# A two-layer gated cross-attention block on one core: the order of transposing turns in one DMA queue

## The reference

```python
x = x + tanh(g_xattn[0]) * L0_xattn(layernorm(x), ctx)      # stage 1: single-head cross-attention
x = x + tanh(g_ffn[0])   * L0_ffn(layernorm(x))             # stage 2: ternary feed-forward
x = x + tanh(g_xattn[1]) * L1_xattn(layernorm(x), ctx, ..)  # stage 3: 16-head cross-attention
x = x + tanh(g_ffn[1])   * L1_ffn(layernorm(x))             # stage 4: FP4 (nvfp4) feed-forward
# L0_ffn: h = gelu(rmsnorm(x) @ ternary(w_up).T); rmsnorm(h) @ ternary(w_down).T     (512 -> 2048 -> 512)
# L1_ffn: h = silu(q(x) @ q(gate).T) * (q(x) @ q(up).T); q(h) @ q(down).T, q = FP4 codes with a scale per 16
```

## Time and profile before

| | |
|---|---|
| median of 3 runs | 1825.38 us (1817.82 to 1830.28) |
| the profiled execution's own time | 1823.66 us |
| its span in the trace | 1821.9 us |
| PE busy | 1371.2 us (75% of the span) |
| DVE busy | 1421.6 us (78%) |
| ACT busy | 692.5 us (38%) |
| POOL busy | 243.9 us (13%) |
| mean granted TensorE clock | 0.892 of full speed |
| busy share of the 16 DMA engines in q1, which holds all of the kernel's transfers | 26.5% |

### The profile page before, as it was taken

One profiled execution on the slowest core, in us unless ns is written; L12 is line 12 of the kernel. 1 busy time (PEld: TensorE's weight loads), 2 busy tenths in 40 slices (PEclk: granted clock), 3 DMA queues, 4 the chain that ended last, 5 costly groups with the idle time before them and its releaser, 6 DMA issues.

```text
span 1821.9 us, 24307 instructions
## 1 busy us (share of the span) xinstructions
PE 1371.2 (75%) x8120; PEld 705.4 (39%) x8120; DVE 1421.6 (78%) x2437; ACT 692.5 (38%) x2105; POOL 243.9 (13%) x197
## 2 busy tenths in 40 slices
PE   5044737799787978698778978797869886988663
PEld 4021315344453436344543345343634453434321
DVE  6988896878787687787787878768777778786695
ACT  2112206451455227441644146422734164425310
POOL 1102200131003200230013100320013001310000
PEclk9556868899889989999999989998999999999888
DMA  9175761042101420233004210142023300420012
GB/s 348 68 243 146 188 143 36 6 88 64 42 1 35 93 59 14 35 62 77 25 7 87 58 48 1 35 93 59 14 35 65 75 24 6 87 58 24 7 24 51
DMA packets 267433, 120.08 MB, mean 66 GB/s; under 512 B 244090, under 2 KB 244602, under 8 KB 265750
## 3 DMA queue, kind: packets, MB, share of 16 engines
q1 hardware_dynamic: 267286, 118.27, 26.5%
HBM read 49.04 MB, written 8.39 MB: 32 GB/s over the span
## 4 chain that ended last, share of the span: by engine, by line
issue 43%; DVE 26%; PE 18%; DMA 4%; SPq 4%; ACT 3%; POOL 2%; POOLq 0%; DVEq 0%; ACTq 0%
PE bank L1075 13%; PE bank L1164 5%; DVE amax L826 2%; DVE pair L835 2%; DVE hid L831 2%; SPq L314 2%; DVE th L868 2%; SPq L303 1%; DVE pair L850 1%; DMA region<-region 1%; ACT region L535 1%; DVE pair L843 1%; DMA hqt<-pair 1%; DVE sc L797 1%; DVE stats L686 1%
## 5 line engine op out<-in xcount | busy, mean ns | idle before, releaser
L1164 PE MATMUL bank<-w_dn,region 128*128 128x512 fp8e4 x1024 | 243.7, 386 | 40.0 <-DMA region<-region 40.0
L1075 PE MATMUL bank<-w_up,xt 128*128 128x512 fp8e4 x1024 | 248.6, 391 | 32.7 <-ACT region L499 17.4
L1075 PE MATMUL bank<-w_gate,xqt 128*128 128x512 bf16 x512 | 147.9, 416 | 122.2 <-DVE th L868 78.4
L508 ACT ACTIVATE th<-bank,half_cg 128x512 f32<-128x512 f32 x128 | 88.0, 687 | 350.2 <-PE bank L1075 350.2
L426 POOL TENSOR_TENSOR region<-g,region 128x512 f16<-128x512 f32 x128 | 178.9, 1402 | 300.9 <-ACT region L499 292.9
L868 DVE SCALAR_TENSOR_TENSOR th<-th,bank 128x512 f32<-128x512 f32 x128 | 87.6, 684 | 138.4 <-ACT th L508 138.3
L535 ACT ACTIVATE region<-bank,nm 128x77 f32<-128x77 f32 x512 | 160.0, 345 | 68.2 <-DVE nm L914 68.2
L1075 PE MATMUL bank<-w_down,hqt 128*128 128x512 bf16 x512 | 134.3, 422 | 56.9 <-DMA hqt<-pair 56.9
L496 ACT ACTIVATE g<-bank 128x512 f32<-128x512 f32 x128 | 76.4, 597 | 247.2 <-PE bank L1075 188.2
L1164 PEld LDWEIGHTS bank<-w_dn,region 128*128 128x128 f16 x1024 | 101.0, 99 | 167.4 <-issue 52.0
L1075 PEld LDWEIGHTS bank<-w_up,xt 128*128 128x128 f16 x1024 | 102.0, 101 | 163.5 <-issue 55.4
(11 more groups left out here) (206 smaller groups left out, 2473.6 us busy)
## 6 DMA issues: line engine op xcount, KB each, us to landing
xin<-in_x SPq DMA_DIRECT2D x16, 512.0 KB, 4.1
out_x<-x SPq DMA_DIRECT2D x16, 512.0 KB, 3.0
region<-in_w_up_t SPq DMA_DIRECT2D x1, 4096.0 KB, 12.9
hid<-in_gate_w SPq DMA_DIRECT2D x4, 1024.0 KB, 5.2
x<-in_gate_w SPq DMA_DIRECT2D x4, 1024.0 KB, 6.1
hid<-in_up_w SPq DMA_DIRECT2D x4, 1024.0 KB, 5.2
x<-in_up_w SPq DMA_DIRECT2D x4, 1024.0 KB, 5.8
hid<-in_down_w SPq DMA_DIRECT2D x4, 1024.0 KB, 4.9
```

Of the source, the lines that this page charges most:

```text
L508: eng.activation(th[:, u % 2, :], bank[4][:, :], ACT.Tanh, scale=half_cg[:, :]).then_inc(sg["th"], 1)
L1075: last = mm(out, lhs, rhs, start=(n == 0), stop=(n == len(pairs) - 1))
L1164: last = mm(bank[2 + t % 2][:, :], ht[i][:, t % 2, f, :], w_dn[:, f, :], start=(f == 0 and i == 0), stop=(f == KF - 1 and i == 1))
```

## The change

In `turns`, which writes the order of SP's queue for a pass, the turn of the first feed-forward's tile 1 is moved ahead of the first code turn `turn_h(g, 0)`, and that of tile 3 ahead of the second one, `turn_h(g, 1)`. Tiles 0 and 2 keep their places. Nothing is added or removed, and no other engine's list changes.

```diff
                 if g1 is not None:
                     turn_ht(g1, 0)
+                    turn_ht(g1, 1)
                 turn_h(g, 0)
                 if g1 is not None:
-                    turn_ht(g1, 1)
                     turn_ht(g1, 2)
+                    turn_ht(g1, 3)
                 turn_h(g, 1)
-                if g1 is not None:
-                    turn_ht(g1, 3)
                 store(g, 0)
```

## The result

| | before | after |
|---|---|---|
| median of 16 runs each | 1821.7 us (1815.69 to 1834.56) | 1810.06 us (1806.84 to 1815.98) |
| the profiled execution's span | 1821.9 us | 1807.6 us |
| mean granted TensorE clock | 0.892 | 0.905 |
| PE busy | 1371.2 us | 1353.0 us |
| DVE busy | 1421.6 us | 1422.8 us |

The ratio is 0.9933 with a 95% interval of 0.9915 to 0.9952. Forecast were 1821 us with a range of 1813 to 1830, a gain of 4.2 us, and 0.95 for staying within 1%. The gain was 11.6 us: still within 1%, but the time lies outside the range, and the gain is nearly three times the 4.2 us of the forecast.

What follows compares the result with a forecast made beforehand. It took a chain going to and fro between PE and DVE to bound the kernel; removing six slot 12 waits gave 1825.4 - 4.2 = 1821 us against the median, with 1813 to 1830 us 8 times in 10.

Steps and rivals of the forecast that it cites:

- the place and the number of the waits: PE's slot 12, first quarter of tile 1's down: six waits of 0.35 to 0.67 us, one per pass except pass 7.
- the second move costs and brings nothing that shows: SP's queue: code turn 1 behind tile 3's turn still lands 5.8 us before PE's slot 20 needs it; cost nothing.
- The size of the term: Slot 12: six waits adding to 3.27 us, plus 6 x 0.15 us for modelled matmul ends, 4.2 us in all.
- Does the end see it? ... I take the whole 4.2 us: Behind slot 12: PE runs in order and DVE, ACT and POOL follow it, so the end gains the full 4.2 us.
- the bounds of 0 and 4.2 us: Gain from slot 12: between 0, if swallowed at some later wait, and the whole 4.2 us.
- The term that the sum had at nothing: PE's clock behind slot 12: by the rows, short waits cost no clock, so filling them gives nothing more.
- The rule weighed: Matmuls back to back keep PE's clock up: filling slot 12 would give at most 2.3 us a pass, 14 us; rows say nothing.
- A late code turn 1: SP's queue behind tile 3's turn, PE's slot 20: 2 us late in each of seven passes, 1835 us; chance 0.04.
- Rival 3: Single instructions last 0.7 us longer or shorter; over seven passes 5 us, 1816 or 1826 us; chance of exceeding the gain 0.12.
- Rival 4: Slot 12: the filled gap also gives back clock, 14 us, 1807 us; chance 0.01.
- The longest such issue was used as a bound: SP's transposes of tile 1: with the longest issue, 3.7 us, and landing, 5.8 us, ready at 391.3, 10 us spare.

Runs made afterwards that it cites:

- before_fill3: Kernel before the change, with 3 matmuls into an unread bank on PE in slot 12 ahead of down, where it waited; 1824.24 us, 0.9999 of before.
- after_five: Changed kernel plus unread matmuls: 12 before gate product fourteen, 16 before tile 3's down4, 8 in attention step 2, 3+3 in steps 18/19, 6 before first up; 1793.61 us.
- after_busy3: Changed kernel with 3 matmuls into an unread bank on PE in slot 12, where it no longer waits; 1827.85 us, 1.0021 of before.
- before_shift: Kernel before the change, with 40 short matmuls (80 instructions) on PE ahead of stage 4's first gate product; 1838.84 us, 1.0077 of before.

## Why the prediction was wrong

**Right**: the place and the number of the waits, that only the six in slot 12 count, that the first move removes them and nothing else waits instead (36.8 us in 3 pieces; I had written about 36.7). Right too that the second move costs and brings nothing that shows: code turn 1 was issued 3.4 us behind its codes instead of 0.1 and was in time. The size of the term holds roughly in the stretches B, 3.1 us in six of them for the pair of traces, against 4.2.

**The step that failed** is "Does the end see it? ... I take the whole 4.2 us", with the bounds of 0 and 4.2 us. It treats what stands behind slot 12 as rigid: shifted, but as long as before. The trace that I had shows that it isn't, beyond the few rows that I had read. In the kernel before the stretches between the same two events last 96 to 103 us, and the runs spread over 12.5 us; I put this spread down to measurement. Much of it goes with the clock, as the executions above show, and the clock hangs on timing: a pass shorter by 0.6 us brought stretches A of 98 and 100 us in place of 98 to 103. That is where some 7 of the 12 us are, and the upper bound of the sum was no bound. The term that the sum had at nothing, the clock behind slot 12, measured 7.6 us in the pair of traces.

**The rule weighed** was asked the wrong question. I looked whether the clock falls in slot 12; it doesn't, and before_fill3 shows that filling that gap gives nothing (1824.2 us). The clock falls in other waits, which the change never touches but moves, and how long it stays down differs from pass to pass. After the same wait of 4.86 us for tile 3's code turn, PE's 16 matmuls in the changed kernel take 6.58 us in one pass and 4.98 us in another (the latter's wait 4.85 us), and behind the 1.40 us that after_five leaves of it 3.63 us:

```profile
866.60 6.58 PE L1074 MATMUL bank<-w_down,hqt 128*128 128x512 bf16 x16 [4.86 <-DMA hqt<-pair]
```

```profile
1064.40 4.98 PE L1074 MATMUL bank<-w_down,hqt 128*128 128x512 bf16 x16 [4.85 <-DMA hqt<-pair]
```

```profile
674.80 3.63 PE L1074 MATMUL bank<-w_down,hqt 128*128 128x512 bf16 x16 [1.40 <-DMA hqt<-pair]
```

The Trainium skill (Perfetto Trace Analysis, Matmul Optimizations) asks for matmuls back to back because the engine scales its power with its use. after_five agrees for the waits of A: with work in them the granted clock is 1.00 there, and the time was 18 us less.

**The rivals.** A late code turn 1 didn't happen. Rival 3, small shifts of either sign, came nearest in form, but I had priced it at 5 us, and for meetings of DVE and POOL; the shifts were larger and the clock's. Rival 4, the clock, had a chance of 0.01 and came nearest in number, with 1807 us. That is in part luck: its mechanism, the filled gap of slot 12, is the one that before_fill3 refutes, and its 14 us came from another wait. But it named the right cost, and the rows against it spoke only of slot 12.

**A cause that was only half named.** The prediction laid the wait to the queue's order, with the 3.49 us of the first issue in the very chain that it quoted. The longest such issue was used as a bound, and why it was that long was not asked. In these traces the wait needs both: the old order and an instruction fetch in that issue. Where either was missing, slot 12 didn't wait.

**Open.** Whose fetch it is was not tested by itself, but the traces speak for PE: q8 has 10 packets in each of the first five passes of the kernel before and of every kernel with at most 12 instructions more on PE, and 11 in all those with 80 or more, and only PE's list was changed between them. By what exactly the timing decides how long the clock stays down was not measured, and so which change of a pass's length helps can't be forecast from these runs. That the change of length acts through the clock is shown by where the time lies and by the two kernels with added matmuls in slot 12; it isn't shown by a pair that differs in the wait alone while the clock is held, since each of the three kernels of the old order with work in the waits lost its wait in the loop as well. So the bare wait's price at an even clock is known only roughly, from the stretches B.

## What to carry to other kernels

Where a loop repeats and PE waits some microseconds in each pass, cut the trace at one event per pass and compare the lengths and granted clocks of the same stretch before summing anything: if they differ, a small edit elsewhere can be worth several times its own size, with either sign, and the range has to hold that. Such a kernel can gain more from work placed in PE's long waits (18 us here, in the third version tried) than from a wait of half a microsecond removed. Test a suspected wait by putting its time back as work. And when a control is meant to hold one thing and leave another, look in its trace whether it did: with work in the waits the two orders, 11 us apart before, were 0 to 3.5 us apart, but the old one had lost its wait too.

## What the runs showed of the hardware

- The length of the same stretch of program went with the granted clock: 98 us at 0.95 to 0.96, 100 at 0.93, 103 to 104 at 0.88 to 0.90, and 95.6 at 1.00 with 14 matmuls more in PE's waits there (after_five). Adding 0.65 us of work a pass moved a kernel from the mixture of 98 and 100 to one with 100 and 104 (after_busy3, 1827.85 us).
- A packet of the instruction queue q8 that falls into the issue of a transposing DMA of 128x2048 went with an issue of 3.0 to 3.7 us, where the others took at most 2.5 us (kernel before, 8 and 56 issues). Pass after pass it met the same issue; 80 instructions added on PE moved it away, 8 did not. A packet that only touched the beginning or the end of an issue left it short (1.6 us in the changed kernel).
- The order of PE's and SP's lists is thus not all that sets their timing: adding instructions to one engine changed the issue time of another engine's DMA by 1.4 us (3.49 us in the kernel before, 2.06 us in before_shift).
